# Three mask stages of a graph network: last part cut at 2500 destinations, one finish for two parts, one mask a head on the other engine

## The reference, cut to what matters

```python
el = jnp.einsum('nhd,hd->nh', h, al)
er = jnp.einsum('nhd,hd->nh', h, ar)
e = jax.nn.leaky_relu(el[src] + er[dst], NEG_SLOPE)
m = jax.ops.segment_max(e, dst, num_segments=N)
ex = jnp.exp(e - m[dst])
s = jax.ops.segment_sum(ex, dst, num_segments=N)
alpha = ex / s[dst]
out = jax.ops.segment_sum(alpha[:, :, None] * h[src], dst, num_segments=N)
```

## Time and profile before

| what | us |
| --- | --- |
| median of 3 runs (2212.75 to 2215.6) | 2215.55 |
| the profiled execution's own time | 2213.15 |
| its span, first to last instruction | 2211.2 |
| PE busy | 1751.3 (79%) |
| DVE busy | 1618.8 (73%) |
| ACT busy | 1409.5 (64%) |
| POOL busy | 302.3 (14%) |
| first eight-head mask stage, from ACT's first mask to the last finishing operation | 420.0 to 765.0 |
| second one | 847.5 to 1192 |
| four-head mask stage | 1897.3 to 2169.0 |

### The profile page before, as it was taken

One profiled execution on the slowest core, in us unless ns is written; L12 is line 12 of the kernel. 1 busy time (PEld: TensorE's weight loads), 2 busy tenths in 40 slices (PEclk: granted clock), 3 DMA queues, 4 the chain that ended last, 5 costly groups with the idle time before them and its releaser, 6 DMA issues. The chain is left out here.

```text
span 2211.2 us, 64081 instructions
## 1 busy us (share of the span) xinstructions
PE 1751.3 (79%) x21987; PEld 1347.2 (61%) x21987; DVE 1618.8 (73%) x3673; ACT 1409.5 (64%) x2346; POOL 302.3 (14%) x457
## 2 busy tenths in 40 slices
PE   3998885389889655988984599998989964688881
PEld 1333334388888635888884366665549963588881
DVE  5988876899999878999998622222332257899997
ACT  0246784799999749999996622221113354899992
POOL 2465500466400011000000000000000001000000
PEclk9999998699999887999997799999989997799996
DMA  1000000011010000101101110000010010000002
GB/s 63 1 1 2 2 3 12 25 38 38 26 38 33 19 26 13 39 26 38 38 26 41 64 38 1 0 0 6 1 29 18 21 63 13 14 20 21 27 15 94
DMA packets 32298, 54.99 MB, mean 25 GB/s; under 512 B 10541, under 2 KB 23626, under 8 KB 31800
## 3 DMA queue, kind: packets, MB, share of 16 engines
q1 hardware_dynamic: 27848, 46.45, 6.3%
q0 software_dynamic: 4208, 5.24, 0.7%
HBM read 43.19 MB, written 8.49 MB: 23 GB/s over the span
## 5 line engine op out<-in xcount | busy, mean ns | idle before, releaser
L1204 PE MATMUL ps<-R,M 128*128 128x132 f16 (+1 forms) x8640 | 809.3, 221 | 202.7 <-DVE M L1117 101.7
L1073 ACT ACTIVATE Rm<-rows,cB 128x1280 bf16<-128x1280 f32 (+1 forms) x832 | 884.3, 1153 | 20.5 <-DVE Mn L1107 13.9
L1204 PEld LDWEIGHTS ps<-R,M 128*128 128x128 f16 x8640 | 729.2, 97 | 245.3 <-issue 115.6
L1212 PE MATMUL ps<-HB,C 128*128 128x66 f16 x6400 | 596.6, 193 | 0.0
L1117 DVE TENSOR_TENSOR M<-Rm,C 128x1280 f16<-128x1280 bf16 (+1 forms) x832 | 555.7, 692 | 41.2 <-ACT Rm L1073 37.5
L1212 PEld LDWEIGHTS ps<-HB,C 128*128 128x128 f16 x6400 | 572.2, 97 | 0.0
L1639 PE MATMUL psA<-R,C 128*128 128x512 f16 (+1 forms) x1200 | 253.8, 351 | 20.9 <-POOL ones L1673 9.3
L546 DVE TENSOR_SCALAR ohc<-cells,near 128x1280 f16<-128x1280 f16 x387 | 213.7, 552 | 53.3 <-PE acc L571 47.3
L571 PE MATMUL acc<-ohc,ohl 128*128 128x420 f16 (+1 forms) x1161 | 244.6, 349 | 1.7 <-issue 0.3
L1120 DVE SCALAR_TENSOR_TENSOR M<-rows,cN,C 128x1280 f16<-128x1280 f32 x128 | 198.0, 1547 | 0.0
L1639 PEld LDWEIGHTS psA<-R,C 128*128 (+1 forms) x1200 | 119.3, 100 | 118.3 <-issue 32.7
(11 more groups left out here) (298 smaller groups left out, 2342.5 us busy)
## 6 DMA issues: line engine op xcount, KB each, us to landing
rows<-rowd SPq DMA_DIRECT2D x32, 640.0 KB, 3.9
rows<-rowd SPq DMA_DIRECT2D x16, 320.0 KB, 3.5
xd<-R SPq DMA_DIRECT2D x4, 640.0 KB, 2.9
xr<-xd SPq DMA_DIRECT2D x20, 128.0 KB, 2.1
xd<-HB SPq DMA_DIRECT2D x1, 2560.0 KB, 8.2
xr<-xd POOLq DMA_DIRECT2D x1, 2560.0 KB, 9.2
R<-in_x SPq DMA_DIRECT2D x1, 2432.0 KB
xr<-in_x SPq DMA_DIRECT2D x19, 128.0 KB, 2.0
```

Of the source, the lines that this page charges most:

```text
L1073: a.activation(Rm[:, s % SG, :], rows[:, p % 2, :], ACT.Relu, bias=cB[:, ds(h + s * nh, 1)]).then_inc(s_R, 1)
L1204: m = pe.matmul(region(p % 2, r), lhsT, rhs, start=first, stop=True, skip_group_check=True)
L1212: m = pe.matmul(both[:, :, cw:2 * cw], C[:, s * NP + p * W + r * P:][:, 0:P], VP[:, s, :, ds(h * cw, cw)], start=False, stop=True, skip_gr ...
```

## The change

Masks of the last part end at its last real destination: `wide(p)` is W, but W - 60 for the last part, in all mask operations of ACT and DVE. PE reads whole tiles as before; the last 60 columns hold what an earlier part left. So that these don't count, `padneg` is added to the exponents of the destination factors of the last tile, which makes these factors zero. `F1` and `F2` become one array `F12`; `tl` gets two halves, one for each part of a pair; the adds are done for each part, and scaling, sum, maximum, reciprocal and mean once for both parts, after the second one's adds: five operations on twice the numbers (the scaling on four times). `stash` and the copy go. `s_E` is raised after the adds, a new `s_fin` after the mean, and ACT waits for `s_fin` of the pair before. With four heads the regions alternate between the two sums, so that a pair lies side by side in `tl`. `(0, 15)` joins `MORE_ON_ACT`: in part 0 of each head of the eight-head layers ACT makes 17 masks and DVE 3 alone.

```diff
-MORE_ON_ACT = {(0, 7), (1, 11)}
+MORE_ON_ACT = {(0, 7), (0, 15), (1, 11)}
...
-                F1, F2 = hp.sb("F1", [P, TH], f32), hp.sb("F2", [P, TH], f32)
+                F12 = hp.sb("F12", [P, 2, TH], f32)
...
                         ch(v.reciprocal(kap[:, :], kap[:, :]))
                         ch.wait()
+                        for q in (tt, tt2):
+                            ch(v.tensor_scalar(q[:, TH - nh:TH], q[:, TH - nh:TH], padneg[:, 0:1], None, ALU.add))
+                        ch.wait()
...
-                    tl = ph.sb("tl", [P, RG, cw if split else 2 * cw], f32)
-                    stash = None if split else ph.sb("stash", [P, TP, dh], f32)
-                    q1 = ph.sb("q1", [P, TP, cw], f32)
-                    rec = ph.sb("rec", [P, TP], f32)
+                    tl = ph.sb("tl", [P, 2, RG, cw if split else 2 * cw], f32)
+                    rec = ph.sb("rec", [P, 2 * TP], f32)
...
+                    wide = lambda p: W - (NP - N if p == PARTS - 1 else 0)
+                    both = lambda q: q[:, :, :, :].rearrange("p s r c -> p (s r c)").rearrange(
+                        "p (t w c) -> p t w c", w=2, c=cw)
...
-                                    a.activation(Rm[:, s % SG, :], rows[:, p % 2, :], ACT.Relu,
+                                    a.activation(Rm[:, s % SG, 0:wide(p)], rows[:, p % 2, 0:wide(p)], ACT.Relu,
                                                  bias=cB[:, ds(h + s * nh, 1)]).then_inc(s_R, 1)
...
-                            hold(a, s_E, q + 2)
+                            hold(a, s_fin, h * (PARTS // 2) + p // 2 + 1)
                             for r, n, part in banks(p % 2, 1):
-                                ins = a.activation(tl[:, r:r + n, :], part, ACT.Copy, scale=1 / LO)
+                                ins = a.activation(tl[:, p % 2, r:r + n, :], part, ACT.Copy, scale=1 / LO)
...
-                                    v.tensor_tensor(M[:, u, :], Rm[:, u, :], Cs, ALU.min).then_inc(s_M if s in ONE else s_cut, 1)
+                                    v.tensor_tensor(M[:, u, 0:wide(p)], Rm[:, u, 0:wide(p)], Cs, ALU.min).then_inc(s_M if s in ONE else s_cut, 1)
...
                             def add():
                                 hold(v, s_tl, q + 1)
-                                for r, n, part in banks(p % 2, 0):
-                                    ch(v.tensor_tensor(tl[:, r:r + n, :], part, tl[:, r:r + n, :], ALU.add))
+                                parts = list(banks(p % 2, 0))
+                                for r, n, part in parts:
+                                    ins = v.tensor_tensor(tl[:, p % 2, r:r + n, :], part, tl[:, p % 2, r:r + n, :], ALU.add)
+                                    if r + n < RG:
+                                        ch(ins)
+                                ins.then_inc(s_E, 1)
 
                             def scale():
+                                hold(v, s_E, q + 3)
                                 ch.wait()
-                                ch(v.tensor_tensor(xv, xv, factor(F2), ALU.mult))
-                                ch(v.tensor_tensor(q1[:, :, :], xu, factor(F1), ALU.mult))
-
-                            def both():
+                                ch(v.tensor_tensor(both(tl), both(tl), factors, ALU.mult))
+
+                            def total():
                                 ch.wait()
-                                v.tensor_tensor(q1[:, :, :], q1[:, :, :], xv, ALU.add).then_inc(s_E, 1)
+                                ch(v.tensor_tensor(both(tl)[:, :, 0], both(tl)[:, :, 0], both(tl)[:, :, 1], ALU.add))
...
-                                ch(v.tensor_tensor(o, q1[:, :, 0:dh], rec[:, :].unsqueeze(2).to_broadcast([P, TP, dh]),
-                                                   ALU.mult))
-
-                            def unstash():
-                                ch.wait()
-                                ch(v.tensor_copy(room[:, 0:TP, ds(h * cw, dh)], stash[:, :, :]))
-
-                            stages = [add, scale, both, weight, inverse, mean]
-                            return stages, [unstash] if not split and p == 1 else []
+                                v.tensor_tensor(room[:, some, ds(h * cw, dh)], both(tl)[:, :, 0, 0:dh],
+                                                rec[:, :].unsqueeze(2).to_broadcast([P, 2 * TP, dh]), ALU.mult).then_inc(s_fin, 1)
+
+                            return [add] + ([scale, total, weight, inverse, mean] if p % 2 else [])
...
-                                        side = r // TP if split else 0
-                                        lhsT = (Mn if side and s in TWO else M)[:, s % SG, (r % TP) * P:(r % TP + 1) * P]
+                                        side, d = (r % 2, r // 2) if split else (0, r)
+                                        lhsT = (Mn if side and s in TWO else M)[:, s % SG, d * P:(d + 1) * P]
```

More of the change, by code:

```diff
@@ L966, in _ @@
                         a.activation(V[:, :], XC[:, :], ACT.Exp, scale=SLOPE).then_inc(s_ex, 1)
-                        a.activation(F1[:, :], tt[:, :], ACT.Exp).then_inc(s_ex, 1)
-                        a.activation(F2[:, :], tt2[:, :], ACT.Exp).then_inc(s_ex, 1)
+                        a.activation(F12[:, 0, :], tt[:, :], ACT.Exp).then_inc(s_ex, 1)
+                        a.activation(F12[:, 1, :], tt2[:, :], ACT.Exp).then_inc(s_ex, 1)
                         def high(k):
@@ L1018, in attention @@
                     ps = [[ph.ps(f"ps{b}{j}", [P, 3 * 2 * XW]) for j in range(NB)] for b in range(2)]
-                    s_R, s_M, s_Mn, s_cut, s_P, s_E, s_tl, s_v = (
-                        ph.sem(n) for n in ("R", "M", "Mn", "cut", "P", "E", "tl", "v"))
+                    s_R, s_M, s_Mn, s_cut, s_P, s_E, s_tl, s_fin, s_v = (
+                        ph.sem(n) for n in ("R", "M", "Mn", "cut", "P", "E", "tl", "fin", "v"))
+                    wide = lambda p: W - (NP - N if p == PARTS - 1 else 0)
+                    both = lambda q: q[:, :, :, :].rearrange("p s r c -> p (s r c)").rearrange(
+                        "p (t w c) -> p t w c", w=2, c=cw)
                     block = ph.enter_context(nc.Block())
@@ L1099, in _ @@
                         v.sem_inc(s_E, 2)
+                        v.sem_inc(s_fin, 1)
                         ch = Chain(v, s_v)
@@ L1105, in low_part @@
                             v.wait_ge(s_cut, (h * PARTS + p) * len(TWO) + TWO.index(s) + 1)
-                            Cs = C[:, s * NP + p * W:s * NP + (p + 1) * W]
-                            v.tensor_tensor(Mn[:, u, :], Cs, M[:, u, :], ALU.subtract).then_inc(s_Mn, 1)
+                            Cs = C[:, s * NP + p * W:s * NP + p * W + wide(p)]
+                            v.tensor_tensor(Mn[:, u, 0:wide(p)], Cs, M[:, u, 0:wide(p)], ALU.subtract).then_inc(s_Mn, 1)
                         def steps(h, p, s0, s1, between=()):
@@ L1116, in steps @@
                                     v.wait_ge(s_P, g + 1)
-                                    v.tensor_tensor(M[:, u, :], Rm[:, u, :], Cs, ALU.min).then_inc(s_M if s in ONE else s_cut, 1)
+                                    v.tensor_tensor(M[:, u, 0:wide(p)], Rm[:, u, 0:wide(p)], Cs, ALU.min).then_inc(s_M if s in ONE else s_cut, 1)
                                 else:
                                     v.wait_ge(s_P, g + 1)
-                                    v.scalar_tensor_tensor(M[:, u, :], rows[:, p % 2, :], cN[:, ds(h + s * nh, 1)], Cs,
+                                    v.scalar_tensor_tensor(M[:, u, 0:wide(p)], rows[:, p % 2, 0:wide(p)], cN[:, ds(h + s * nh, 1)], Cs,
                                                            ALU.is_gt, ALU.mult).then_inc(s_M, 1)
@@ L1132, in evacuation @@
                             q = h * PARTS + p
-                            factor = lambda Fq: Fq[:, :].rearrange("p (t h) -> p t h", h=nh)[
-                                :, p * TP:(p + 1) * TP, ds(h, 1)].to_broadcast([P, TP, cw])
-                            xu, xv = (tl[:, 0:TP, :], tl[:, TP:2 * TP, :]) if split else (tl[:, :, 0:cw], tl[:, :, cw:2 * cw])
+                            some = slice(p // 2 * 2 * TP, (p // 2 * 2 + 2) * TP)
+                            factors = F12[:, :, :].rearrange("p w (t h) -> p t w h", h=nh)[:, some, :, ds(h, 1)].to_broadcast(
+                                [P, 2 * TP, 2, cw])
@@ L1155, in weight @@
                             def weight():
-                                hold(v, s_E, q + 3)
-                                ch(v.tensor_scalar(rec[:, :], q1[:, :, dh], 1e-30, None, ALU.max))
+                                ch.wait()
+                                ch(v.tensor_scalar(rec[:, :], both(tl)[:, :, 0, dh], 1e-30, None, ALU.max))
                             def inverse():
@@ L1165, in mean @@
                                 ch.wait()
-                                ch(v.tensor_tensor(o, q1[:, :, 0:dh], rec[:, :].unsqueeze(2).to_broadcast([P, TP, dh]),
-                                                   ALU.mult))
```

(18 more changed lines are left out.)

2 lines of the change are left out of this document (removed).

## The result

| what | before | after |
| --- | --- | --- |
| median of ten runs each, us | 2214.07 | 2219.86 |
| profiled execution's span, us | 2211.2 | 2217.7 |
| first eight-head mask stage, us (first mask of ScalarE to last finishing operation) | 345.0 | 348.4 |
| second eight-head mask stage, us | 344.3 | 348.4 |
| four-head mask stage, us | 271.7 | 269.7 |

A forecast was written before the change was run, and what follows sets the result against it. ACT's own pace was taken to bound the eight-head layers, with waits for DVE in the four-head layer. Eight-head +4.7, four-head -2.6, ends +3.1, before exponentials +1.0 gave +6.2 us: 2222 us, range 2205 to 2232.

The forecast's parts named there:

- ACT's own pace sets the eight-head layers: Eight-head layers: ACT, not DVE, is the bound before and after; 0.44 us a head more, +4.7 us with the old wait gone.
- The old hidden wait goes: Eight-head layers: ACT's 0.15 us a head wait for DVE, hidden in its busy time, disappears.
- The narrow mask: Last part's masks: 60 columns fewer save ACT 0.051 us a mask, -0.81 us a head in the eight-head layers.
- The merged finishing: DVE's finishing for two parts: multiplication 1.54, addition 0.85, mean 0.83 us; -0.6 us a head, all in one part.
- No stop in part 0: Eight-head part 0: the finishing burst causes no new ACT wait; DVE needs 8.5 us while ACT delivers six masks in 7.5.
- The four-head layer: Four-head mask stage: +1.5 us from waits in pairs, -4.1 from narrow masks, together -2.6 us; parts alternate near 17.4 and 15.1.
- Ends: Ends of the three mask stages: uncovered finishing grows by 0.9 us per eight-head layer and 1.3 in the four-head, +3.1 us.
- Before the exponentials: Chain before the exponentials: two small additions and a wait on DVE cost 0.35 us in each of three layers, +1.0 us.
- Stalls at the four-head jump stay: Four-head loop's jump back: DVE's stalls of 2.8 to 3.1 us are kept, none added to the sum.
- The direction of the extra mask: (0, 15) goes to ACT, as the diff says, not from ScalarE to VectorE as announced: +1.253 us a head on ACT.
- rival 1: Averages rule: slots carry DVE over the burst, waiting within stages vanishes, four-head parts take 15.65 us; -10.5 us, 2205; chance 0.10.

The follow-up runs named there:

- e3: Kernel before with only (0, 15) added to the masks ACT makes, nothing else; 2234.33 us, ratio 1.0096.
- e1: Changed kernel without the extra mask: (0, 15) given back to DVE, 16 and 16 masks a head on ACT; 2210.64 us, ratio 0.9988.
- e2: Kernel before with only the narrow masks in the last part and the padneg additions; 2200.94 us, ratio 0.9945.
- e6: Changed kernel with only (0, 7) in MORE_ON_ACT: ACT makes 16 + 15 masks a head in the eight-head layers; 2190.97 us, ratio 0.9887.
- e5: Changed kernel with (1, 11) moved from ACT to DVE, so ACT makes 17 + 15 masks a head; 2201.68 us, ratio 0.9942.
- e4: Changed kernel with full-width masks, the old set of masks on ACT and no padneg additions: merged finishing only; 2224.16 us, ratio 1.0052.
- e7: Kernel before with the four-head layer's finishing stages spread two masks apart, same work in another order; 2207.00 us, ratio 0.9961.
- e8: Eight-head layers as in e6; four-head layer with narrow masks and the old single finishing, spread over the masks; 2184.13 us, ratio 0.9861.

## Why the prediction was right

It said 2222 us, by a sum of +6.2; the runs gave 2219.86 and +5.8. By its steps:

- **ACT's own pace sets the eight-head layers.** Held: e3 alone, and no idle time after. A head went from 42.14 to 42.44 us in the first layer and from 42.07 to 42.44 in the second; I had +0.29, measured +0.30 and +0.37. The stages less their ends grew by (3.4 - 0.9) + (4.0 - 0.9) = 5.6 us against 4.7.
- **The old hidden wait goes.** Held by half: the run of 17 took 21.32 us, where ACT's own pace gives 14 x 1.253 + 2 x 1.203 + 1.30 = 21.25, so 0.07 of the 0.15 us is left. ACT's own work of a head after is 17 x 1.253 + 16 x 1.203 + 1.54 = 42.1, and 0.35 us are left over it, 0.5 before. Most of that was never the finishing's: it lies just before the evacuations, where the traces of e1, e2 and e6 have ACT wait 0.17 to 0.24 us for PE's products.
- **The narrow mask**: 0.051 us taken, 0.046 and 0.052 measured.
- **The merged finishing**: 1.54, 0.85 and 0.83 taken from a float32 row on 1024 numbers, 1.53, 0.85 and 0.83 measured. Pricing by the nearest row and a slope was exact here.
- **No stop in part 0.** Held with 17 masks. e1 shows how near it was: one mask less on ACT, and ACT waits 0.66 us.
- **The four-head layer**: parts near 17.4 and 15.1 expected, 17.6, 17.2 and 15.1, 14.5 found; the stage less its end fell by 2.0 + 1.4 = 3.4 us against 2.6.
- **Ends**: +3.1 taken; from ACT's last mask to the last finishing operation it was 8.78, 8.78 and 8.14 us, and is 9.69, 9.68 and 9.52: +3.2.
- **Before the exponentials**: 0.35 a layer taken, 0.40 measured in the first.
- **Stalls at the four-head jump stay.** Held; after the change DVE stands still there too:

```profile
2032.69 0.46 DVE L1112 TENSOR_TENSOR Mn<-C,M 128x580 f16<-128x580 f16 x1
2036.08 0.89 DVE L1122 TENSOR_TENSOR M<-Rm,C 128x640 f16<-128x640 bf16 x2 [2.93 <-PE ps L1203]
```

- **The direction of the extra mask**: as the diff has it, not as announced. ACT has 848 masks, before 832. The announced direction is e5's, and it is 18 us faster than the change.

That the total came so near is in part luck: the eight-head layers missed by +0.9 us and the four-head layer by -0.8. And of the 2 us between 2222 and 2219.86, 1.5 come from the median before, 2215.55 of three runs and 2214.07 of ten.

The weak place was rival 1: its chance of 0.10 was right to be low (e4 shows that a smaller sum alone gives nothing), but I did not see that the same spare time can be had by *placing* work. Its pace for the four-head layer, DVE's average of 15.65 us a part, is what e7 reached by spreading (15.7), still above ACT's own 15.1. The merged finishing, which it was a forecast for, gave 17.2 to 17.6 and 15.1 instead.

## What to carry to other kernels

When two engines are both nearly always busy (here DVE and ACT, 98.7% and 99.6% of a window in the eight-head layers, 94.7% and 93.1% in the four-head layer) and hand work to each other through a few slots, compare their sums part by part, not over the whole loop: work that is made cheaper but put into one place can cost (e4, +11 us), and the same work spread out can gain (e7, -8.5). After such a change, balance anew in each part: here the right set of masks (e6) turned +6 us into -25. A part of a change that pays for itself (the narrow masks, -12 us) is only seen when it is run alone.

## What was not expected of the hardware

A loop's jump back cost DVE 2.8 to 3.1 us and ACT 1.9 to 2.0 us in the four-head layer, and nothing to be seen in the eight-head loops; the profile puts DVE's stop down to ACT's mask or to PE's product, though the mask had been done since 2027.9 in the earlier trace rows. What tells it from a wait for data is the DMA view: packets of an instruction queue, 31 in the stage and 14 once the loop is written out. Writing three rounds out gained 0.26%, in before and in e8 alike.
